# Final normalization of a fused attention and mixture-of-experts layer: where the two partial sums are added, and how tokens' rows lie in DRAM

## The reference

```
x = layernorm(x + attention(x))         # 16 heads of 64, rotary, causal
g = softmax(x @ gate); keep the top 3 of 16 experts, scaled to sum 1
y = sum over the 3 chosen experts of g_e * (relu(x @ W1_e + b1_e) @ W2_e + b2_e)
out = layernorm(x + y)                  # mean and variance over the 256 features, eps 1e-5
```

## Time and profile before

| | us |
|---|---|
| median of the runs | 1890.16 |
| runs | 1882.93, 1890.16, 1892.10 |
| profiled execution, its own time | 1883.92 |
| its span | 1881.9 |
| attention and routing, to the first gather | 1397.1 |
| last scatter issued | 1822.3 |
| first instruction of the combine phase | 1828.9 |
| end | 1881.9 |

### The profile page before, as it was taken

The page is one execution under the profiler, slowest core; times in us unless marked ns, Lnnn a source line. Parts: engine busy times, 40 slices in busy tenths (PEclk is TensorE's granted clock), DMA queues, the critical chain, the costliest instruction groups (busy, mean ns, idle before and its releaser), DMA issues. The chain is left out here.

```text
span 1881.9 us, 33776 instructions
## 1 busy us (share of the span) xinstructions
PE 1718.3 (91%) x9587; PEld 1282.2 (68%) x9588; DVE 1362.3 (72%) x3170; ACT 742.6 (39%) x1583; POOL 1261.6 (67%) x1086
## 2 busy tenths in 40 slices
PE   5489999999999999999999999998679999999970
PEld 4357667766766676667667666754349999999960
DVE  3368888888888888888888888865974445444435
ACT  3134444445445544444444445544442222222213
POOL 2157778777877776787778688843347777777753
PEclk8689999999999999999999999999559999999985
DMA  9866556655655675556667545614944444444447
GB/s 313 282 189 183 144 168 201 192 152 162 182 155 180 200 206 144 169 173 175 190 195 198 158 152 164 179 47 141 376 117 72 72 74 71 73 72 72 73 82 236
DMA packets 185043, 300.41 MB, mean 160 GB/s; under 512 B 23104, under 2 KB 82496, under 8 KB 184912
## 3 DMA queue, kind: packets, MB, share of 16 engines
q1 hardware_dynamic: 161344, 267.23, 48.0%
q0 software_dynamic: 21504, 30.29, 9.9%
q10 hardware_dynamic: 2064, 1.31, 0.2%
HBM read 186.84 MB, written 111.67 MB: 159 GB/s over the span
## 5 line engine op out<-in xcount | busy, mean ns | idle before, releaser
L733 ACT ACTIVATE prob<-b_ps 128x512 f32<-128x512 f32 (+3 forms) x768 | 354.2, 488 | 358.3 <-PE b_ps L570 263.9
L497 POOL TENSOR_TENSOR acc<-acc,prob 128x1024 f32<-128x1024 f32 (+1 forms) x192 | 352.5, 1836 | 6.4 <-POOL acc L497 3.6
L569 PE MATMUL b_ps<-q,k 128*128 128x512 f32 (+3 forms) x768 | 295.6, 389 | 5.7 <-ACT prob L733 3.5
L470 POOL TENSOR_TENSOR roped<-rot 128x512 f32<-128x512 f32 x128 | 174.6, 1364 | 179.8 <-DVE rot L856 179.0
L562 PE MATMUL a_ps<-k,q 128*128 128x512 f32 (+3 forms) x768 | 265.3, 382 | 20.4 <-DMA k<-scratch_hilo 11.0
L838 DVE CUSTOM_DVE_ANT_0 masked<-a_ps,causal 128x128 bf16<-128x128 f32 (+3 forms) x512 | 237.1, 478 | 51.9 <-PE a_ps L562 44.4
L651 PE MATMUL y_ps<-prob,v_sb 128*64 128x512 f32 (+3 forms) x1536 | 273.7, 491 | 0.0
L1571 DVE TENSOR_SCALAR hT<-h_ps,b1T 128x128 f32<-128x128 f32 x448 | 126.1, 344 | 197.0 <-PE h_ps L1487 142.1
L570 PE MATMUL b_ps<-q,k 65*128 65x512 f32 (+3 forms) x768 | 264.2, 348 | 0.0
L1461 POOL DMA_INDIRECT scratch_sum<-y,dst_i x112 | 177.7, 1586 | 95.2 <-ACT y L1536 85.1
L886 DVE RECIPROCAL inv<-inv 128x128 f32<-128x128 f32 x256 | 232.1, 929 | 8.5 <-ACT inv L774 6.2
(11 more groups left out here) (258 smaller groups left out, 2472.6 us busy)
## 6 DMA issues: line engine op xcount, KB each, us to landing
q<-scratch_hilo SPq DMA_DIRECT2D x192, 256.0 KB, 4.6
k<-scratch_hilo SPq DMA_DIRECT2D x192, 256.0 KB, 5.2
scratch_hilo<-hi SPq DMA_DIRECT2D x64, 512.0 KB, 4.0
scratch_hilo<-lo SPq DMA_DIRECT2D x64, 512.0 KB, 4.5
w_sb<-scratch_wsplit SPq DMA_DIRECT2D x32, 512.0 KB, 3.6
w<-in_L_ffn_W_dram SPq DMA_DIRECT2D x32, 512.0 KB, 9.9
wv_sb<-scratch_wsplit SPq DMA_DIRECT2D x16, 512.0 KB, 6.4
xT<-scratch_xsplit SPq DMA_DIRECT2D x6, 1024.0 KB, 6.8
```

What stands on the lines that cost most here:

```text
L497: nc.gpsimd.tensor_tensor(sums, old, probs(q), ALU.add).then_inc(m["sum_p"], 1)
L569: nc.tensor.matmul(out, k1[s][:, h, js], q1[s][:, h, qs], start=True, stop=False, skip_group_check=True)
L733: nc.scalar.activation(probs(q)[:, h, :], b_ps[:, h, 0:w], ACT.Exp).then_inc(exp_done[h], 1)
```

## The change

Four things are done.

- **Layout.** In `xn`, `sum0` and `sum1` token (t, p) is now row 32 p + t. A partition's tiles lie one after the other in DRAM. The stores of `xn` and of `sum0`, the gate columns and the row numbers in `src_i` and `dst_i` follow. The output keeps its layout.
- **Loads moved.** Still in the expert block, SP waits for the last scatter into `sum0` and loads `sum0` in six groups of 4, 4, 8, 8, 4, 4 tiles into `x1a`/`x1b`. POOL, after both scatter chains, waits for each group and adds `sum1` to it in place with an accumulating DMA. `got0`, `got1` and the adds on POOL are gone.
- **Order on DVE.** `scales(g)` follows `moments(g)` at once; there is no look-ahead by a group.
- **Small parts.** ACT issues one root of a constant first. Tiles 27 and 31 are normalized by DVE instead of ACT.

```diff
+def token_sums(dram, i):
+    return dram[f"sum{i}"][0:NTOK, :].rearrange("(p t) d -> p t d", p=P)
...
-            xn = dram["xn"][:, E_:E_ + D].rearrange("(b t p) d -> b p t d", b=B, p=P)
+            xn = dram["xn"][:, E_:E_ + D].rearrange("(p b t) d -> b p t d", b=B, p=P)
...
+SIZES = (4, 4, 8, 8, 4, 4)
...
-            first = dram["sum0"].rearrange("(t p) d -> p t d", p=P)
+            first = token_sums(dram, 0)
...
-            link(V.scalar_tensor_tensor(out=place, in0=which, scalar=float(P), in1=row, ...))
+            link(V.scalar_tensor_tensor(out=place, in0=row, scalar=float(TILES), in1=which, ...))
...
+        @block.sync                      # expert_phase
+        def _(sp):
+            sp.wait_ge(ys_st[0], 16 * SLOT_TILES // SUMS)
+            for g in range(len(SIZES)):
+                rows, here = sum_rows(g)
+                sp.dma_start(here, token_sums(dram, 0)[:, rows, :]).then_inc(S["first_in"][g], 16)
...
             for s in range(2):
                 pool.wait_ge(ys_st[s], 16 * SLOT_TILES // 2)
+            for g in range(len(SIZES)):
+                rows, here = sum_rows(g)
+                pool.wait_ge(S["first_in"][g], 16)
+                pool.dma_start(here, token_sums(dram, 1)[:, rows, :], accum_op=ALU.add).then_inc(S["both_in"][g], 16)
...
-            for g in range(GROUPS):      # combine_phase, SP
-                for i in range(SUMS):
-                    sp.dma_start(got[i][:, rows(g), :], ...).then_inc(ld[g], 16)
...
-        @block.gpsimd
-        def _(pool):
-            for g in range(GROUPS):
-                pool.wait_ge(ld[g], 32)
-                nc.gpsimd.tensor_tensor(got[0][:, rows(g), :], got[0][:, rows(g), :], got[1][:, rows(g), :], ALU.add)
...
+            nc.scalar.activation(r[:, 2, 0:1], eps[:, 0:1], ACT.Sqrt)
...
-                dve.wait_ge(m["c_added"], g + 1)
+                dve.wait_ge(S["both_in"][g], 16)
...
-            moments(0)
             for g in range(GROUPS):
-                if g + 1 < GROUPS:
-                    moments(g + 1)
+                moments(g)
                 scales(g)
+                normalize(g)             # by DVE: tiles 27 and 31
```

More of the change, by code:

```diff
@@ L910 @@
 AHEAD = 4
+SIZES = (4, 4, 8, 8, 4, 4)
+ENDS = [sum(SIZES[:g + 1]) for g in range(len(SIZES))]
 SUMS = 2
@@ L1404, in _ @@
             link(V.tensor_copy(which, src_i[:]))
-            link(V.scalar_tensor_tensor(out=place, in0=which, scalar=float(P), in1=row, op0=ALU.mult, op1=ALU.add))
+            link(V.scalar_tensor_tensor(out=place, in0=row, scalar=float(TILES), in1=which, op0=ALU.mult, op1=ALU.add))
             V.tensor_copy(src_i[:], place)
@@ L1433, in expert_phase, with sum_rows @@
         LOOPS = SLOT_TILES // XIN - 1
+        def sum_rows(g):
+            half, t = (S["x1a"] if ENDS[g] <= 2 * TB else S["x1b"]), ENDS[g] - SIZES[g]
+            return slice(t, t + SIZES[g]), half[:, t % (2 * TB):t % (2 * TB) + SIZES[g], :]
+        @block.sync
[4 more added lines that the diff above has]
+                sp.dma_start(here, token_sums(dram, 0)[:, rows, :]).then_inc(S["first_in"][g], 16)
         def done(t):
@@ L1593, in combine_phase @@
 def combine_phase(nc, A, dram, S, out):
-    SIZES = (4, 8, 8, 8, 4)
-    ENDS = [sum(SIZES[:g + 1]) for g in range(len(SIZES))]
     GROUPS = len(SIZES)
@@ L1600, in sb @@
             return ctx.enter_context(nc.sbuf_tensor(name, shape, dt))
-        got = [sb(f"got{i}", [P, TILES, D], F32) for i in range(2)]
         stats = sb("stats2", [P, TILES, 6], F32)
@@ L1606, in combine_phase @@
         eps = sb("eps2", [P, 1], F32)
-        names = "c_added c_chain c_eps c_var c_std c_rs c_out c_stored".split()
+        names = "c_chain c_eps c_var c_std c_rs c_out c_stored".split()
         m = {k: ctx.enter_context(nc.semaphore(k)) for k in names}
-        ld = [ctx.enter_context(nc.semaphore(f"got_ld{g}")) for g in range(GROUPS)]
         block = ctx.enter_context(nc.Block())
@@ L1614, in rows, with by_act @@
             return slice(ENDS[g] - SIZES[g], ENDS[g])
+        def by_act(t):
+            return t < TILES - 8 or t % 4 < 3
         @block.sync
@@ L1618, in _ @@
             for g in range(GROUPS):
-                for i in range(SUMS):
-                    sp.dma_start(got[i][:, rows(g), :],
-                                 dram[f"sum{i}"].rearrange("(t p) d -> p t d", p=P)[:, rows(g), :]).then_inc(ld[g], 16)
-            for g in range(GROUPS):
+                half, t = (S["x1a"] if ENDS[g] <= 2 * TB else S["x1b"]), (ENDS[g] - SIZES[g]) % (2 * TB)
                 sp.wait_ge(m["c_out"], ENDS[g])
-                sp.dma_start(out_v[:, rows(g), :], got[1][:, rows(g), :]).then_inc(m["c_stored"], 16)
+                sp.dma_start(out_v[:, rows(g), :], half[:, t:t + SIZES[g], :]).then_inc(m["c_stored"], 16)
             sp.wait_ge(m["c_stored"], 16 * GROUPS)
-        @block.gpsimd
-        def _(pool):
-            for g in range(GROUPS):
-                pool.wait_ge(ld[g], 32)
-                nc.gpsimd.tensor_tensor(got[0][:, rows(g), :], got[0][:, rows(g), :], got[1][:, rows(g), :], ALU.add)\
-                    .then_inc(m["c_added"], 1)
         @block.scalar
@@ L1636, in _, with roots @@
             act.wait_ge(m["c_eps"], 1)
-            for g in range(GROUPS):
+            nc.scalar.activation(r[:, 2, 0:1], eps[:, 0:1], ACT.Sqrt)
+            def roots(g):
                 act.wait_ge(m["c_var"], g + 1)
@@ L1640, in _ @@
                     .then_inc(m["c_std"], 1)
+            for g in range(GROUPS):
+                roots(g)
                 act.wait_ge(m["c_rs"], g + 1)
                 for t in range(ENDS[g] - SIZES[g], ENDS[g]):
-                    nc.scalar.activation(got[1][:, t, :], got[0][:, t, :], ACT.Identity, bias=r[:, 4, t:t + 1],
-                                         scale=r[:, 3, t:t + 1]).then_inc(m["c_out"], 1)
+                    if by_act(t):
+                        nc.scalar.activation(token_rows(S, t), token_rows(S, t), ACT.Identity, bias=r[:, 4, t:t + 1],
+                                             scale=r[:, 3, t:t + 1]).then_inc(m["c_out"], 1)
         @block.vector
@@ L1678, in scales, with normalize @@
                                        op1=ALU.mult).then_inc(m["c_rs"], 1)
-            moments(0)
+            def normalize(g):
+                for t in range(ENDS[g] - SIZES[g], ENDS[g]):
+                    if not by_act(t):
+                        dve.wait_ge(m["c_rs"], g + 1)
+                        V.tensor_scalar(token_rows(S, t), token_rows(S, t), r[:, 3, t:t + 1], r[:, 4, t:t + 1], ALU.mult,
+                                        ALU.add).then_inc(m["c_out"], 1)
             for g in range(GROUPS):
-                if g + 1 < GROUPS:
-                    moments(g + 1)
+                moments(g)
                 scales(g)
+                normalize(g)
 def post_ln_block(nc, A, dram, out):
@@ L1699, in post_ln_block @@
         S.update(zeros=sb("zeros", [P, D], F32), sums_in=ctx.enter_context(nc.semaphore("sums_in")))
+        for name in ("first_in", "both_in"):
+            S[name] = [ctx.enter_context(nc.semaphore(f"{name}{g}")) for g in range(len(SIZES))]
         with ExitStack() as inner:
```

8 lines of the change are left out of this document (4 added, 4 removed).

## The result

| | before | after |
|---|---|---|
| time, median of 4 runs | 1890.47 us | 1899.96 us |
| lowest to highest | 1882.93 to 1892.1 | 1898.53 to 1901.84 |
| ratio to before, 95% interval | | 1.0056 [1.0038, 1.0074] |
| profiled execution, its span | 1883.92, 1881.9 | 1898.53, 1896.5 |

The change makes the kernel 9.5 us slower by the medians, and the interval of the ratio leaves out 1. The forecast was 1885.3, faster by 3.1; the time lies at the upper end of the range, on the wrong side.

What follows compares the result with a forecast made beforehand. Bound: 52.9 us from barrier to end, ACT setting the pace at the end. Release 1847.3 + 31.5 = 1878.8, 3.1 below 1881.9; set on the runs' mean, 1888.4 - 3.1 = 1885.3 us, range 1875 to 1900.

Steps and rivals of the forecast that it cites:

- The step that failed: Combine phase's start: last group of `sum0` seen at 1843.7, last add issued by 1845.3, barrier 2.0 us, release at 1847.3.
- The 1.1 and 2.9 us: Barrier times read in the earlier trace (1396.07 to 1397.13, 1826.1 to 1829.0), from which 2.0 us was taken.
- They don't hold up DVE: Adds end about 1857.8, but group 2 is there by 1847.6 (wanted at 1854), group 3 by 1853.4 (wanted at 1859).
- The early start of SP's loads: SP's first load of `sum0` issues at 1824.2 instead of 1828.93, with data flowing from 1826.4.
- The work behind the barrier: DVE's and ACT's combine work from release to end, with all data there: 31.5 us, store included, against 52.9 before.
- An add's cost: DMA time of accumulating loads: 0.64 us per tile, twice a plain copy's 0.32, bounded above by a scatter's 1.1.
- the dear adds of the slow rival: At POOL's wait for the last `sum0` group: adds cost 1.1 us at equal turns, end 1894.4, 12.5 us more; chance 0.15.
- two to one: Queue sharing while `sum0` loads: two tiles of `sum0` per tile of adds, 0.64 us per `sum0` tile, 12.8 us for twenty.
- equal turns: Rival on queue sharing: 20 tiles cost 0.32 + 0.64 each, barrier opens at 1853.7, end 3.3 us more; chance 0.15.
- the first rival: Loads go ahead of the adds while `sum0` loads: barrier opens at 1840.9, end 1872.4, 9.5 us less; chance 0.22.
- the rival of the far rows: Rows 32 KB apart slow the experts' scatters; at 7.5 us to landing, 44 us more; chance 0.04.
- the lost look-ahead: At group 2 of the combine phase, ACT waits 1.4 us, once, for DVE's moments of 8 tiles.

Runs made afterwards that it cites:

- e5: Changed kernel with the accumulating loads of groups 0 to 2 left ahead of the barrier and those of groups 3 to 5 behind it; 1889.8 us, one run.
- e6: Changed kernel with the first sum left out and the second loaded by six plain POOL loads without waits; 1878.47 us, one run.
- e3: Kernel before with only the DRAM layout of `xn` and both sums changed; 1887.21 us, 0.9994 of before.
- e2: Kernel before with only DVE's order changed, scales right behind their own moments; 1884.06 us, 0.9966 of before.
- e7: e1 with the second sum's first two groups loaded plainly by SP behind the barrier and added by DVE; 1884.83 us, 0.9979 of before.
- e9: e7 with SP's queue reordered: three first-sum groups ahead of the barrier, then the two DVE adds, then the rest; 1880.5 us, 0.9958 of before.
- e4: Changed kernel without the accumulating loads, DVE waiting for the first sum's loads alone; 1870.64 us, one run.
- e1: Changed kernel with POOL's six accumulating loads moved behind the barrier into the combine block; 1878.13 us, 0.9952 of before.
- e10: e1 with the layout of the kernel before, so loads and adds go in 1 KB pieces; 1882.38 us, 0.9957 of before.
- e11: e1 with SP's six loads of `sum0` moved behind the barrier too; 1881.97 us, 0.9958 of before.

## Why the prediction was wrong, by its own steps

**The step that failed** is the end of the sentence "The combine phase starts when the *last* group of `sum0` has landed, plus one issue and the barrier". POOL issues its last add, and then the barrier took not 2.0 us but 13.5. The combine phase starts when the last *add* has landed, plus 1.6 to 1.7 us (after, e5 and e6), because POOL's DRAIN at the end of its block lasts until POOL's own transfers have landed. The 1.1 and 2.9 us that I took the 2.0 from the earlier trace rows come from ends of blocks at which POOL had no transfer under way (for the 2.9, an explicit wait had emptied its queue of scatters first), so those rows could not have shown it. Their use as a bound for an end of block with six DMAs under way was the mistake: no row bounded it, and I named none above 2.9.

In numbers, from the last scatter's issue:

| | forecast | measured |
|---|---|---|
| first load of SP | 1.9 | 1.8 |
| first add issued | 6.1 | 8.1 |
| first bytes of the adds | 7.9 | 12.6 |
| last group of `sum0` seen by POOL | 21.4 | 23.8 |
| last add issued | 23.0 | 24.6 |
| last add landed | 35.5 | 36.4 |
| release | 25.0 | 38.1 |
| release to end | 31.5 | 31.2 |
| tail | 56.5 | 69.3 |

The miss is 12.8 us: 11.5 by the barrier, 1.6 by the later last add, -0.3 by the work behind. (The 1.6 is small by luck, as the sharing of the queues below shows.) My own landing of the adds, 1857.8, with 2.0 us for the barrier and 31.5 of work, gives 1891.3, 9.4 above 1881.9: the result, had the one rule been the other way. "They don't hold up DVE" was true of the groups and false of the barrier.

**The other steps.** The early start of SP's loads came as said. The work behind the barrier, 31.2 us, was right, ACT's gaps with it (it starts group 0 at +3.4 and group 1 at +6.9, as forecast). An add's cost was right: 0.63 us per tile at 207 GB/s against 0.64, so the dear adds of the slow rival did not occur. That rival came close in the end time (12.5 us slower against 9.5) by the wrong mechanism: it has POOL see the last group of `sum0` at 1858.6, 36 us after the last scatter, and it was 23.8. I had given the slow side 0.20 in all, with no part of it for what happened.

**How the queues shared** was wrong, and already in the reading of before. The earlier trace rows count ten microseconds, but ACT's queue had packets in only some seven of them (none from 1320 to 1322, 10 after 1329). Where both had work, from 1323 to 1328, it was one packet each (packets, MB, share):

```profile
q1 hardware_dynamic: 822, 1.09, 59.0%
q10 hardware_dynamic: 820, 0.84, 47.4%
```

After the change it is the same. From 1837 to 1840 the adds, though two were issued by 1837.1, have next to nothing; from 1840 to 1847 they take turns with the loads:

```profile
q1 hardware_dynamic: 153, 1.02, 97.2%
q0 software_dynamic: 3, 0.01, 2.1%
```

```profile
q0 software_dynamic: 258, 0.99, 70.6%
q1 hardware_dynamic: 243, 0.92, 35.1%
```

So two to one never held. The Trainium skill's rule that I cited in the prediction for equal turns ("DMA: Bandwidth & Descriptors", section "Queues, rings and completion order") agrees with both stretches, and what I held against it from the earlier trace rows was a window that averaged over an idle queue.

That the last group of `sum0` still came only 2.4 us late (23.8 against 21.4) is luck. Equal turns from the forecast's start of the adds were priced at 6.4 us more. But the adds began 4.7 us later than forecast: 2.0 because the first group landed and was seen later, the rest because the first bytes of an add came 4.5 us after its issue and not 1.8 as a scatter's. By 1840, 3.14 MB of the 4.19 of `sum0`, 24 of 32 tiles, had gone ahead alone, where I had 12. In that the first rival, loads ahead of the adds, was three quarters right. A load cost 0.37 us per tile (35.0% of 34 us for 32 tiles), 0.05 more than forecast.

**The layout** cost the experts nothing: a scatter lands in 3.8 us with rows 34 or 32 KB apart, after as before (e3), and the rival of the far rows is gone. By one profile each it was worth 2.2 us of tail on its own (e3); the runs don't tell it from nothing.

**The order on DVE** was, with hindsight, the best part of the change for its size: 5.7 us of tail alone (e2). I had booked its cost (1.4 us for the lost look-ahead) beside its gain only within the sum behind the barrier.

**What stays open.** Why POOL's DRAIN waits for transfers and SP's doesn't, the traces don't say, nor whether a block of another engine with DMAs of its own on the software queue would do the same; it wasn't tried. And why the adds' first bytes come so late isn't shown: full DMA engines are the likely cause, since the second batch of adds in e5 (issued at 1856.91, the engines idle) moved its first bytes after 1.5 us, and ACT's store of the earlier trace rows, no accumulation at all, after 3.9 us beside a full queue.

## What to carry to other kernels

Before work is put in front of a block's end "because it only has to be issued", ask what that end waits for. Here POOL's transfers were waited for to their landing and SP's weren't, so POOL's long transfers belong behind the barrier, where the same six lines turned +0.56% into -0.48%.

In a sum that has "issued, then free" in it, price the other reading too, "landed, then free". It costs one line, and here it would have given +9.4 us. Where a long wait names only the line that closes a block, ask the trace for that line: the DRAIN of the engine that held it stands there with its duration. A ratio in which two queues share is to be read only over the time in which both have packets. And when a stage starts with data that arrive in turn, it's the first group's place in the queue that counts: e7 and e9 differ in little else, and the tails are 57.2 and 48.7.

## What the runs showed of the hardware, unexpected

- The end of POOL's block waited for the DMAs of its queue, plain or accumulating, in a DRAIN of 11.94 to 16.23 us (2.43 with nothing under way), and opened 1.6 to 1.7 us after the last had landed; with SP's last load 9 us from landing (e4) SP's DRAIN took 0.12 us and the barrier opened at +6.8, where it opens with nothing under way (+6.7).
- Two queues with work took one packet each: 822 to 820 for two hardware queues (before), 258 to 243 for the software queue against a hardware queue (after).
- A DMA issued while another queue filled the DMA engines moved its first bytes 4.1 to 4.7 us after its issue (first adds of after, e1, e5, e7, e9, e10, e11) or 3.9 (ACT's store, before); into idle engines it took 1.3 (e6) and 1.5 (e5).
- Accumulating loads from DRAM ran at 207 GB/s in pieces of 4 and 8 KB and at 203 in pieces of 1 KB, while plain loads gained from large pieces (423 against 350).
- The issue of ten loads in 1 KB pieces kept SP for 19.08 us (before), in large pieces for 4.86 (e3); of three loads for 6.72 (e10) and 1.50 to 2.76 (e7, after, e1, e4, e5).
- A short DVE instruction on 128 x 4 (0.16 us) took up to 4.48 us beside a POOL add of 128 x 2048.
